# First group reordered, one weight tile quantized per body over two groups, and two groups' linear layer in the last phase

## The reference, cut to what matters

```python
xn = layernorm(x)                                  # x: 4096 tokens x 1024 features
q, k, v = heads((xn @ Wq + bq) / 8), heads(xn @ Wk + bk), heads(xn @ Wv + bv)   # 16 heads of 64
ret = (q @ k.T) * exp(decay_h * (i - j)) * (i >= j)          # over 1024 tokens
attn = (ret / clip(abs(ret.sum(-1)), 1)) @ v
g = groupnorm_per_head(attn) * gn_w + gn_b
y = (silu(xn @ Wg + bg) * g) @ Wo + bo
wq, ws, w_ts = quantize_nvfp4(w_f)     # w_ts = max(abs(w_f)) / (448 * 6): needs all of w_f first
xq, xs, _   = quantize_nvfp4(xn, x_ts) # blocks of 16: scale rounded to e4m3, values to e2m1
f = (xq*xs) @ (wq*ws).T * (x_ts * w_ts) + bias
out = x + y + f
```

## Time and profile before

| | us |
|---|---|
| median of three runs | 2232.05 (2230.95 to 2232.88) |
| the profiled execution | 2231.07 |
| its span, first to last instruction | 2228.9 |
| TensorE busy | 2093.5 |
| VectorE busy | 1534.4 |
| ScalarE busy | 689.3 |
| GpSimd busy | 641.3 |
| mean granted TensorE clock | 0.972 of full |

### The profile page before, as it was taken

How to read it: one execution, slowest core, us unless ns; L and a number is a source line. 1 busy time by engine, 2 the same in 40 slices (tenths; PEclk the granted TensorE clock), 3 DMA queues, 4 the chain that set the end, 5 groups by cost and what they waited for, 6 DMA issues and landing times.

```text
span 2228.9 us, 51250 instructions
## 1 busy us (share of the span) xinstructions
PE 2093.5 (94%) x18047; PEld 1066.7 (48%) x18098; DVE 1534.4 (69%) x4379; ACT 689.3 (31%) x1318; POOL 641.3 (29%) x456
## 2 busy tenths in 40 slices
PE   5687888989899999999999999999999999999999
PEld 3343444444454545555545455554554555545444
DVE  8587878999966666666676766666666666666742
ACT  5555451322133223222322322223222322322210
POOL 1222232233232332223332232332332223323321
PEclk8888999999899999999999999999999999999999
DMA  7656733432333332323333233233333322333323
GB/s 309 214 190 219 258 110 95 144 108 91 94 119 118 101 106 90 100 89 104 118 110 109 90 99 108 77 118 118 108 108 90 99 90 94 119 118 99 104 75 123
DMA packets 180244, 269.30 MB, mean 121 GB/s; under 512 B 117184, under 2 KB 117312, under 8 KB 180160
## 3 DMA queue, kind: packets, MB, share of 16 engines
q1 hardware_dynamic: 180160, 268.19, 37.7%
HBM read 201.04 MB, written 37.75 MB: 107 GB/s over the span
## 4 chain that ended last, share of the span: by engine, by line
PE 74%; DVE 17%; DMA 3%; issue 2%; ACT 1%; SPq 1%; POOL 0%; DVEq 0%; ACTq 0%
PE mm L1257 46%; PE mm L1199 7%; PE tp L1199 7%; PE mm L1208 4%; DMA ftile<-in_w_f 2%; PE tp L1267 2%; PE four L1307 2%; PE four L1320 2%; PE tp L1295 1%; DVE xa L807 1%; PE four L1280 1%; DVE xa L808 1%; DVE state L1004 1%; DVE xa L802 1%; DVE wo L896 1%
## 5 line engine op out<-in xcount | busy, mean ns | idle before, releaser
L1257 PE MATMUL mm<-xnT,wring 128*128 128x512 f16 x6144 | 1379.2, 383 | 14.4 <-ACT qT L620 14.1
L1257 PEld LDWEIGHTS mm<-xnT,wring 128*128 128x128 f16 x6144 | 603.1, 99 | 720.3 <-issue 44.1
L651 ACT ACTIVATE work<-four,gs 128x64 f32<-128x64 f32 x512 | 158.5, 414 | 575.5 <-DVE gs L1031 575.5
L512 POOL TENSOR_TENSOR yT<-gn,gate 128x512 f32 (+1 forms) x64 | 82.8, 1293 | 881.2 <-ACT gn L662 881.2
L1018 DVE BATCH_NORM_STATS2 gst<-four 128x6 f32<-128x64 f32 x512 | 73.6, 217 | 215.4 <-PE four L1320 215.4
L1199 PE MATMUL mm<-wo,yT 128*128 128x512 f16 x864 | 194.1, 381 | 0.1
L495 POOL TENSOR_TENSOR qparts<-qT,qparts 128x512 f16<-128x512 f32 x64 | 78.5, 1227 | 372.0 <-ACT qT L620 371.8
L495 POOL TENSOR_TENSOR kparts<-kT,kparts 128x512 f16<-128x512 f32 x64 | 83.0, 1297 | 234.5 <-ACT kT L620 234.5
L1199 PE MATMUL tp<-wo,yT 128*128 128x512 f16 x672 | 149.6, 379 | 0.0
L1199 PEld LDWEIGHTS mm<-wo,yT 128*128 (+1 forms) x864 | 82.3, 98 | 98.7 <-issue 1.9
L620 ACT ACTIVATE vT<-mm,consts,down 128x512 f32<-128x512 f32 x64 | 49.8, 778 | 230.4 <-PE mm L1257 230.4
(11 more groups left out here) (194 smaller groups left out, 2710.5 us busy)
## 6 DMA issues: line engine op xcount, KB each, us to landing
wring<-parts SPq DMA_DIRECT2D x252, 512.0 KB, 3.5
xt<-in_x SPq DMA_DIRECT2D x34, 512.0 KB, 3.6
out<-res SPq DMA_DIRECT2D x32, 512.0 KB, 3.0
parts<-wo SPq DMA_DIRECT2D x28, 512.0 KB, 8.1
res<-in_x SPq DMA_DIRECT2D x28, 512.0 KB, 3.6
ftile<-in_w_f SPq DMA_DIRECT2D x16, 512.0 KB, 4.7
parts<-wring SPq DMA_DIRECT2D x8, 512.0 KB, 7.1
probs<-in_x SPq DMA_DIRECT2D x5, 512.0 KB, 3.8
```

The costliest lines, as they stand in the source:

```text
L512: nc.gpsimd.tensor_tensor(hi, gn[:], gate[:, u], ALU.mult)
L651: last = nc.scalar.activation(work[:, c * P + h * HD:c * P + (h + 1) * HD], ao[h][:, c * VW:c * VW + HD], ACT.Identity, bias=gs[:, 1, g:g ...
L1257: last = MM(mm[n % 2][:], wring[:, n, wj, k, :], xnT[:, parity, xj, k, :], start=(j == 0), stop=(j == 3 * KT - 1))
```

## The change

- FIRST: SP loads tiles of w_f into two buffers in turn (`ftile`, `res`), some at the head of a body and one towards its end; each waits for the maximum of the tile two before. SP's fourth slice load stands ahead of the transposing DMAs. VectorE makes the batch's scales before it quantizes x (bodies 1 to 3), finds maxima at two places instead of three, and mixes the splits differently. TensorE's `sum_slices` move: the first into the transpositions of START, the second behind `project(0, 0)`, the third behind `scores(0)` and `project(1, 1)`; `transpose_g(0)` moves behind `attend_within(1)`.
- SECOND and a new phase THIRD (group 2) each quantize one tile of w_f per body. Neither has the linear layer; MIDDLE is groups 3 to 7. The same names run the phase THIRD on each engine, and GpSimd's `add_biases` stands in THIRD as in SECOND.
- The quantized x of group 1 is stored to memory (`xq1`, 1 MB) ahead of SECOND and loaded back ahead of TAIL into a part of `xnT`.
- TAIL: each body does the late linear layer of two tiles, j = 0 (group 0; banks `sc`, buffer `xt`) and j = 1 (group 1; banks `ao`, buffer `ftile`). `late_ready` and `late_stored` are raised twice ahead.

```diff
 BATCHES = PAIRS // 2 + 1
-F_TILES = ((0, 1, 2), (3, 4, 5), (6, 7), ())
+F_TILES = (((0,), (1,)), ((2, 3), (4,)), ((5, 6), (7,)), ((), ()))
...
-START, FIRST, SECOND, MIDDLE, TAIL = range(5)
-BODIES = (0, CH, CH, CH * (GROUPS - 2), CH)
+START, FIRST, SECOND, THIRD, MIDDLE, TAIL = range(6)
+QUANTIZE = (SECOND, THIRD)
+BODIES = (0, CH, CH, CH, CH * (GROUPS - 3), CH)
...
-    "late_ready": (1, 0, 0, 0, 1)
+    "late_ready": (2, 0, 0, 0, 0, 2)
...
+        late_x = [xqT[:, 0], xnT[:, 1, 0].rearrange("p k t -> p (k t)").bitcast(BF16).rearrange(
+            "p (c k t) -> p c k t", c=CH, k=KT)]
+        late_bufs = [xt, ftile]
+        late_banks = [sc, ao]
                 def load_f_raw(t):
-                    if t:
-                        sp.wait_ge(s["f_max"], at("f_max", START, 0, t))
-                    sp.dma_start(ftile[:], a["w_f"][t * P:(t + 1) * P, :]).then_inc(s["f_loaded"], 16)
+                    if t > 1:
+                        sp.wait_ge(s["f_max"], at("f_max", START, 0, t - 1))
+                    elif t == 1:
+                        sp.wait_ge(bias_sum, 1)
+                    sp.dma_start(f_bufs[t % 2][:], a["w_f"][t * P:(t + 1) * P, :]).then_inc(f_in[t % 2], 16)
...
-                    w("late_stored", 0)
-                    sp.wait_ge(s["x_loaded"], at("x_loaded", TAIL, 0, 0))
-                    sp.dma_start(xt[:], a["out"][ds(q * P, P), :]).then_inc(s["x_loaded"], 16)
-                    w("late_ready", 1)
-                    sp.dma_start(a["out"][ds(q * P, P), :], xt[:]).then_inc(s["late_stored"], 16)
+                    for j in range(2):
+                        late_rows = a["out"][ds(q * P + j * GROUP, P), :]
+                        w("late_stored", j)
+                        if j == 0:
+                            sp.wait_ge(s["x_loaded"], at("x_loaded", TAIL, 0, 0))
+                        sp.dma_start(late_bufs[j][:], late_rows).then_inc(s["late_loaded"], 16)
+                        w("late_ready", j + 1)
+                        sp.dma_start(late_rows, late_bufs[j][:]).then_inc(s["late_stored"], 16)
                     w("out_ready", 1)
                     sp.dma_start(a["out"][rows, :], res[:]).then_inc(s["out_stored"], 16)
...
                         load_slice(0, n)
+                    load_fs(F_TILES[i][0])
                     if i == 0:
                         load_raw(1, 6)
                         load_raw(1, 7)
-                    next_f()
                     load_slice(0, 2)
                     if i == 0:
                         for c in range(4, SLICES):
                             store_parts(0, c)
+                    else:
+                        pass_on(range(0, 4))
+                    load_slice(0, 3)
                     move_x_parts()
-                    load_slice(0, 3)
-                    if i > 0:
-                        pass_on(range(0, 4))
                     w("xq_ready", 1)
                     move_x()
...
                     load_slice(1, 0)
                     load_slice(1, 1)
-                    next_f()
                     pass_on(range(4, SLICES))
                     load_slice(1, 2)
-                    next_f()
+                    load_fs(F_TILES[i][1])
                     load_slice(1, 3)
                     return
+                if phase in QUANTIZE:
+                    sp.wait_ge(s["f_max"], at("f_max", SECOND, 0, 0))
                 w("out_stored", 0)
                 sp.dma_start(res[:], a["x"][rows, :]).then_inc(s["res_loaded"], 16)
-                if phase == SECOND:
-                    w("f_max", 0)
-                    load_f(0)
+                if phase in QUANTIZE:
+                    load_f()
                     load_slice(0, 0)
                     load_slice(0, 1)
                     move_x_parts()
                     load_slice(0, 3)
                     load_slice(1, 0)
                     load_slice(1, 1)
-                    move_f(0)
-                    load_f(1)
+                    move_f()
                     load_slice(1, 2)
                     load_slice(1, 3)
                     move_x()
                     w("out_ready", 1)
                     sp.dma_start(a["out"][rows, :], res[:]).then_inc(s["out_stored"], 16)
-                    move_f(1)
                     return
                 for n in range(4):
...
                 store_parts(0, c)
-            for phase in (FIRST, SECOND, MIDDLE, TAIL):
+            for phase in (FIRST, SECOND, THIRD, MIDDLE, TAIL):
+                if phase == SECOND:
+                    sp.wait_ge(s["xq_moved"], at("xq_moved", SECOND, 0, 0))
+                    sp.dma_start(a["xq1"], xqT[:, 1].rearrange("p c k t -> p (c k t)")).then_inc(xq1_kept, 16)
+                if phase == THIRD:
+                    sp.wait_ge(xq1_kept, 16)
+                if phase == TAIL:
+                    sp.wait_ge(s["attn_full"], at("attn_full", TAIL, 0, 0))
+                    sp.dma_start(late_x[1].rearrange("p c k t -> p (c k t)"), a["xq1"]).then_inc(xq1_back, 16)
                 run_phase(sp, phase, body)
...
                 if phase == TAIL:
-                    w("x_loaded", 1)
-                    w("late_full", 2)
-                    for h in range(2):
-                        V.scalar_tensor_tensor(half(xt, h), sc[h], ffn_scale, half(xt, h), ALU.mult, ALU.add)\
-                         .then_inc(s["late_added"], 1)
-                    w("late_added", 2)
-                    V.tensor_copy(ls[:, 18:19], ls[:, 15:16]).then_inc(s["late_ready"], 1)
+                    for j in range(2):
+                        w("late_loaded", j + 1)
+                        w("late_full", 2 * j + 2)
+                        for h in range(2):
+                            o = half(late_bufs[j], h)
+                            V.scalar_tensor_tensor(o, late_banks[j][h], ffn_scale, o, ALU.mult, ALU.add)\
+                             .then_inc(s["late_added"], 1)
+                        w("late_added", 2 * j + 2)
+                        V.tensor_copy(ls[:, 18:19], ls[:, 15:16]).then_inc(s["late_ready"], 1)
                     emit_half(w, 0, "mm0", 1)
                     emit_linear(w, 0, "mm1", 1)
...
                     w("xn_ready", 1)
-                    quantize_scales(xt, x_ts, x_r6)
-                    w("xq_moved", 0)
-                    quantize_half(xt, 0)
                     if i == CH - 1:
                         in_scales(weight_scales)
                     if i:
                         scale_batch()
-                        split_lo(i + 1, range(0, 6))
+                    quantize_scales(xt, x_ts, x_r6)
+                    w("xq_moved", 0)
+                    if i:
+                        split_lo(i + 1, range(0, 4))
+                    quantize_half(xt, 0)
+                    if i:
+                        split_lo(i + 1, range(4, 6))
                     mask_scores(0)
+                    if i:
+                        split_lo(i + 1, range(6, SLICES))
+                    quantize_half(xt, 1)
                     if i == 0:
                         scale_batch()
-                    quantize_half(xt, 1)
-                    if i:
-                        split_lo(i + 1, range(6, SLICES))
                     states(0)
-                    find_f_max()
+                    find_f_max(F_TILES[i][0])
                     if i == 0:
                         split_lo(1, range(0, 4))
                     group_norm(0)
-                    find_f_max()
                     if i == 0:
                         split_lo(1, range(4, 6))
                     mask_scores(1)
                     if i == 0:
                         split_lo(1, range(6, SLICES))
                     group_norm(1)
-                    find_f_max()
+                    find_f_max(F_TILES[i][1])
...
                 quantize_half(xt, 1)
-                if phase == SECOND:
-                    f_scales(0)
+                if phase in QUANTIZE:
+                    f_scales()
                 mask_scores(0)
-                if phase == SECOND:
+                if phase in QUANTIZE:
                     f_half(0)
                 states(0)
-                if phase == SECOND:
+                if phase in QUANTIZE:
                     f_half(1)
                 group_norm(0)
-                if phase == SECOND:
-                    f_scales(1)
                 mask_scores(1)
-                if phase == SECOND:
-                    f_half(0)
                 states(1)
                 emit_half(w, 0, "mm0", 5)
                 if phase == MIDDLE:
                     emit_linear(w, 0, "mm1", 5)
                 group_norm(1)
-                if phase == SECOND:
+                if phase in QUANTIZE:
                     emit_half(w, 1, "mm1", 5)
                     emit_done(w, "mm1_free", 5)
-                    f_half(1)
                 if phase == MIDDLE:
                     emit_half(w, 1, "t1", 4)
...
                 w("xn_ready", t + 1)
+                if t == 2:
```

(31 more changed lines are left out.)

96 lines of the change are left out of this document (50 added, 46 removed), and 8 rows, old and new, of the table PER.

## The result

The changed kernel takes **2214.1 us** (2213.2 to 2216.5, 4 runs) against 2231.6 (2231.0 to 2232.9, 4 runs) of the kernel before on the same chip: ratio 0.9925, 95% interval 0.991 to 0.994. The forecast was 2198 (2174 to 2222): the sign was right and the time lies in the range, but the gain is half of what I said, 17 us in place of 34. The profiled execution has a span of 2212.2 us.

What follows compares the result with a forecast made beforehand. TensorE was taken to bound the steady part, VectorE's work the first group's later bodies. Groups -50, tail +51, first group -35 sum to -34: 2231.07 to 2197, median 2198 us, range 2174 to 2222.

Steps and rivals of the forecast that it cites:

- term A: Second and third group: eight bodies of 62.5 us, 500 in place of 549.8 us, so -50 us.
- term C: First group: earlier start, shorter first body, and bodies 1 to 3 shorter by 8, 7 and 4 us; -35 us in all.
- term B: Tail: first body +15 us, three others 36 us longer together; +51 us, of which 13.4 is moved work.
- no tail wait: Rival, chance 0.04: the tail does not wait as counts say, or loads come far earlier; +17 there, time 2164.
- slow tail: Rival, chance 0.06: TensorE's clock stays at 1.2 GHz through the tail; +60 there, total +26, time 2258.
- 60.7 + 0.95 + 0.9 = 62.5: Second- and third-group body in us: TensorE's work, its wait for mask_scores(0), and its wait before the gate's transposition.
- short waits lose clock: Rival, chance 0.09: second- and third-group mask waits near 2 us also cost 2.4 us of clock; gain there -23, time 2225.
- VectorE's own work, 55.0, 53.3 and 50.3 us, becomes the bound: First group, bodies 1 to 3: VectorE's work plus remaining waits gives 65, 60 and 58.5 us; -8, -7, -4.
- the scales: First group, bodies 1 to 3: scales ahead of quantizing x end ScalarE's 25.0 us of waits; bodies -8, -7, -4 us.
- the sums: First group: moved sums make the start some 5 us earlier and take 7 us of square waits from body 0.
- the second buffer: First group, body 0: w_f tile read elsewhere shrinks TensorE's second-mask wait from 9.93 to some 7 us; -3 us.
- held by transfers: Rival, chance 0.10: transfers hold the first group, which gains only 8 us; time 2225.

Runs made afterwards that it cites:

- e_tail_count: Changed kernel with TensorE waiting in the tail for late_ready j-1 in place of j: 2188.6 us, ratio 0.9791 to the kernel before.
- e_stats_first: Changed kernel with VectorE's group_norm(0) ahead of f_half(1) in the second and third group: 2208.8 us, ratio 0.989 to the kernel before.
- e_group_order: Changed kernel, second and third group: group_norm(0) ahead of f_half(1), mask_scores(0) ahead of f_scales(), states(0) ahead of f_half(0): 2197.6 us, 0.9846 to the kernel before.
- e_bias_early: Changed kernel with GpSimd's add_biases behind split(3), not gate_y(0), in the second and third group: 2233.2 us, ratio 1.0 to the kernel before.
- e_pool_narrow: Changed kernel with GpSimd's x_lo on 64 of 1024 columns in the second and third group: 2205.2 us, ratio 0.988 to the kernel before.
- the nine kernels: The changed kernel and eight others with the same first group; their second group begins at 288.7 to 292.6 us, 290.6 on average.
- e_less_vector: Changed kernel with x's second half quantized on 64 of 512 columns in the first group's third and fourth body: 2213.6 us, 0.991 to the kernel before.
- e_first_order: Changed kernel, VectorE in first group's third and fourth body: mask_scores(0), half of x, states(0), other half, splits 4 to 7: 2216.0 us, 0.9929 to kernel before.
- e_scales_late: Changed kernel with the scales again behind quantize_half(xt, 0) in bodies 1 to 3 of the first group: 2214.6 us, 0.9916 to the kernel before.
- e_best_b: Changed kernel with tail and group orders changed, plus group_norm(1) ahead of splits 6 and 7 in the first body: 2163.0 us, 0.9685 to kernel before.

## Why the prediction was wrong, and where it held

The gain came out 17.3 us too small in the spans: 9.4 us in term A, 7.2 in term C, 0.5 in term B and 0.2 in the bodies between. Terms A and C missed in the same direction, so nothing cancelled between the terms.

**Term B, the tail: +51 forecast, +51.5 measured.** The counts were read rightly, and e_tail_count shows the mechanism. Its pieces: TensorE stood 12.2 us at the head (forecast 13.3), where the load of 1 MB landed in 5.2 us and not in 6. The first body ends 13.6 us later against the last full body's end (15), and the other three take 38.0 us more (36): that the sum fits to 0.5 us is in part luck. Before the third linear half stand 6.3, 6.8 and 6.5 us (6.4), and the clock takes 2.1, 2.6 and about 3 us (2.1). The rival "no tail wait" is out by these idles, and "slow tail" by the clock, which is 1.00 again in the window behind the slow matmuls.

**Term A, the groups: -50 forecast, -40.6 measured.** The mechanism was right: the waits of 3.46 and 4.41 us went, mask and transposition wait 1.06 and 0.85 us (0.95 and 0.9). The step that failed is the sum "60.7 + 0.95 + 0.9 = 62.5", which came out 1.2 us too low on average of the eight bodies. Two things were missing. One is a third wait, 0.64 us, for the first output addition. In the middle groups GpSimd adds the biases early; here it does so behind gate_y(0), VectorE waits 3.68 us for it, and I had not followed GpSimd's order. The other is that an idle costs more than its length even at a clock of 1.00: a body less its waits is 61.23 us with three of them, 60.98 with two (e_stats_first), 60.93 with one (e_group_order), and 64.08 less twice 1.74 (start to start of a linear half) = 60.6 with none. What the engine does in the extra 0.3 to 0.6 us no run here shows. And the forecast took GpSimd for an engine beside the path, with VectorE's time beside it only in a rival: e_bias_early and e_pool_narrow show it in VectorE's loop. My rival "short waits lose clock" is out: the windows' clock is 1.00.

**Term C, the first group: -35 forecast, -27.8 measured** (-26 on the average of the nine kernels). The start and the first body were right (second body at 96.3, forecast 98), though the wait for the second mask in the first body shrank only from 9.93 to 8.11 us, where I had 7. Bodies two to four came out at 68.4, 62.5 and 61.6 for 65, 60 and 58.5. The step that failed is "VectorE's own work, 55.0, 53.3 and 50.3 us, becomes the bound", and it failed in two ways.

The first is the size. VectorE is busy 56.5, 56.5 and 54.7 us in these bodies, 9.1 more in all, and the bodies came out 8.9 longer than forecast: I took its length from a kernel in which it was less crowded. In the fourth body the same instructions, with one search for the maximum of 1.2 us more, are busy 54.74 us in place of 50.31. Four splits, before and after, in the view that groups instructions (busy us, mean ns of one | idle before):

```profile
L896 DVE SCALAR_TENSOR_TENSOR wo<-wf,o_found,wo 128x1024 f16<-128x1024 f32 x4 | 6.9, 1772 | 3.4 <-ACT wo L589 3.4
```

```profile
L916 DVE SCALAR_TENSOR_TENSOR wo<-wf,o_found,wo 128x1024 f16<-128x1024 f32 x4 | 8.7, 2228 | 0.0
```

The trace says that GpSimd stretches them. One of the four splits took 3.15 us, where such a split takes 1.28 alone, beside GpSimd's `x_lo`:

```profile
256.18 3.15 DVE L916 SCALAR_TENSOR_TENSOR wo<-wf,o_found,wo 128x1024 f16<-128x1024 f32 x1
...
255.13 3.11 POOL L539 TENSOR_TENSOR xhl<-xt,xhl 128x1024 f16<-128x1024 f32 x1
```

Summed over bodies two to four, what VectorE's instructions took beyond the short ones of their own form (counted from 0.1 us up) is 23.8 us before and 32.3 after, and every one of these instructions overlaps one of GpSimd's. That is 8.5 of the 9.1 us. It is a reading of two traces; no run took GpSimd's work away in the first group.

The second is the bound itself. By its sum VectorE does not bound these bodies: e_less_vector took 1.3 and 2.8 us off its busy time and no time came of it. What e_less_vector and e_first_order show in its place is the loop of VectorE up to a mask and TensorE behind it, with the second mask close behind the first. So the match of 9.1 and 8.9 us is no proof that the busy sum sets the time.

Inside the term the shares were wrong too: the scales, which I counted on for bodies two to four, are worth nothing (e_scales_late); the sums brought about 4 us, not 10; the second buffer with its order, for whose waits I gave 3, brings 7 to 9. Some 14 us of the gain were undone by no single edit; whether VectorE's order of splits and halves, TensorE's later transposition or SyncE's order gives them stays open. So does what in the second body's 68.4 us would go with the 7.7 us wait for squares; e_best_b shows only that moving group_norm(1) ahead of two splits does not pay.

The rival "held by transfers" (term C -8) is out for the group as a whole. But in the first body the DMA engines are busy 0.93 of 65.0 us, and 0.93 x 65.0 = 60.4 us is the floor that the prediction worked out: about 5 us at most are left there for any order.

Two readings in the prediction are a little off, and nothing hangs on them: 33.9 less 33.1 is 0.8 us and not 0.95, and the four bodies of the first group are 79.5 us above 50.3 each, not 78.

## What to carry to other kernels

Ask of a wait not only how long it is but which loop it lies in: two engines that hand work to each other once a body form a loop, and an edit pays only if it shortens the longest one. In the first group three edits moved a wait of 6 to 9 us from one place to another and gained nothing; in the second and third, changes of VectorE's order alone gained 17 us with the same work. When a phase takes on more pieces, read every count its waits ask for again: one that was never asked for before cost 27 us here, and `j - 1` in place of `j` mends it. And an engine's busy time is taken from the schedule it was measured in: in a denser one the same instructions took longer here.
